# A fused linear-attention and windowed-attention stack on one core: the next rows turned inside an iteration's last products, the order of VectorE's and GpSimd's work rearranged, and a third pair of heads weighed by ScalarE in odd iterations

## What is computed

```python
xn = _layernorm(x)
# linear path, 16 heads of 32
q = softmax(_ln(xn) @ Wq + bq); k = softmax(_ln(xn) @ Wk + bk); v, p = split(_ln(xn) @ W_in)
k = (1 - smear) * k + smear * k_shifted_by_one_row
attn = tril(einsum(q, k) * decay);  o = (attn / (attn.sum(-1) + eps)) @ v
s = _ln(silu(p) * o @ W_out)
# window path, two layers, 8 heads of 64, windows of 128 rows
for l in range(2):
    h = shift_token(x); q, k, v = split(h @ wqkv[l]); q, k = rotary(l2norm(q), l2norm(k))
    x = x + softmax(q @ [k_before, k_own] + mask) @ [v_before, v_own] @ wo[l]
    h = _ln(shift_token(x)); a, g = split(h @ w1[l] + b1[l]); x = x + (a * gelu(g)) @ w2[l] + b2[l]
out = x0 + s * silu(x)
```

## Time and profile before

| | us |
|---|---|
| median of 3 runs | 2095.14 (2093.2 to 2096.72) |
| the profiled execution, device time | 2084.63 |
| its span, first to last instruction | 2082.8 |
| TensorE busy | 1938.6 (93%) |
| VectorE busy | 1791.2 (86%) |
| ScalarE busy | 1153.7 (55%) |
| GpSimd busy | 973.5 (47%) |

### The profile page before, as it was taken

How to read it: one execution, slowest core, us unless ns; L and a number is a source line. 1 busy time by engine, 2 the same in 40 slices (tenths; PEclk the granted TensorE clock), 3 DMA queues, 4 the chain that set the end, 5 groups by cost and what they waited for, 6 DMA issues and landing times.

```text
span 2082.8 us, 49017 instructions
## 1 busy us (share of the span) xinstructions
PE 1938.6 (93%) x15282; PEld 1668.4 (80%) x15282; DVE 1791.2 (86%) x5354; ACT 1153.7 (55%) x2734; POOL 973.5 (47%) x941
## 2 busy tenths in 40 slices
PE   5899999999999999999999999999999999999997
PEld 3788888888888888888787888877888778888786
DVE  6898898899898899889878888888988988888885
ACT  4465565566555556556545555555555655555553
POOL 3454544555554555554344434444444545344440
PEclk9999999999999999999999999999999999999998
DMA  5011000000000000100221011110111111111100
GB/s 191 18 31 31 19 29 25 28 20 30 28 19 25 30 19 29 30 19 30 69 64 37 28 36 33 30 40 27 36 35 29 34 33 30 35 31 32 38 22 24
DMA packets 81153, 72.78 MB, mean 35 GB/s; under 512 B 13484, under 2 KB 74344, under 8 KB 81096
## 3 DMA queue, kind: packets, MB, share of 16 engines
q1 hardware_dynamic: 81096, 72.05, 11.4%
HBM read 42.64 MB, written 16.78 MB: 29 GB/s over the span
## 4 chain that ended last, share of the span: by engine, by line
PE 47%; DVE 27%; issue 14%; POOL 8%; ACT 2%; DVEq 1%; SPq 0%; POOLq 0%; DMA 0%; ACTq 0%
PE bank L1403 31%; PE bank L1408 9%; PE bank L1415 6%; POOL inv_norm L648 6%; DVE prob L1002 4%; DVE prob L988 4%; ACT xT L767 2%; DVE sq_sum L1284 2%; DVE qk_sum L1296 2%; POOL k_carry L707 2%; DVE mix_work L1248 1%; DVE mix_work L1269 1%; DVE row_inv L997 1%; DVE row_min L988 1%; DVE h_n L1241 1%
## 5 line engine op out<-in xcount | busy, mean ns | idle before, releaser
L1403 PE MATMUL bank<-hT_n,w_s 128*128 128x128 f32 x3072 | 417.8, 288 | 17.5 <-ACT gel L888 16.8
L1403 PEld LDWEIGHTS bank<-hT_n,w_s 128*128 128x128 f32 x3072 | 379.2, 198 | 49.7 <-ACT gel L888 24.2
L798 ACT ACTIVATE prob<-prob,row_min 128x256 f32<-128x256 f32 x512 | 256.6, 503 | 160.9 <-DVE row_min L988 160.6
L1408 PE MATMUL bank<-wqkv_s,xT 128*128 128x512 f32 x1152 | 314.7, 408 | 15.7 <-DVE xT L1179 12.8
L691 POOL TENSOR_TENSOR rot_other<-raw,rot_t 128x256 f32<-128x256 f32 x256 | 187.7, 765 | 235.8 <-ACT raw L767 235.8
L648 POOL TENSOR_TENSOR inv_norm<-sq_clip,half_neg 128x16 f32<-128x16 f32 x64 | 218.4, 3412 | 91.4 <-DVE sq_clip L1287 91.3
L1408 PEld LDWEIGHTS bank<-wqkv_s,xT 128*128 128x128 f32 x1152 | 205.7, 190 | 67.3 <-DVE xT L1179 24.5
L988 DVE CUSTOM_DVE_ANT_0 prob<-bank,table,inv_norm 128x256 f32<-128x256 f32 x512 | 226.0, 478 | 2.3 <-issue 2.3
L1002 DVE TENSOR_SCALAR prob<-prob,row_inv 128x256 f32<-128x256 f32 x512 | 207.5, 447 | 9.1
L1403 PE MATMUL bank<-w_s,hid 128*128 128x256 f32 x768 | 195.2, 384 | 0.5 <-DVE hid L1332 0.5
L767 ACT ACTIVATE pT<-bank 128x512 f32<-128x512 f32 x256 | 145.0, 606 | 72.1 <-PE bank L1415 71.9
(11 more groups left out here) (182 smaller groups left out, 4261.5 us busy)
## 6 DMA issues: line engine op xcount, KB each, us to landing
k_prev<-k_carry SPq DMA_DIRECT2D x32, 224.0 KB, 2.5
x_s<-in_L_attn_x SPq DMA_DIRECT2D x32, 128.0 KB, 2.1
rot_s<-in_rotary SPq DMA_DIRECT2D x64, 64.0 KB, 2.0
rows_normalised<-xh SPq DMA_DIRECT2D x32, 128.0 KB, 1.7
y_n<-rows_normalised SPq DMA_DIRECT2D x32, 128.0 KB, 2.1
x_between_layers<-x SPq DMA_DIRECT2D x32, 128.0 KB, 1.7
s_between_passes<-s_out SPq DMA_DIRECT2D x32, 128.0 KB, 1.7
x_s<-x_between_layers SPq DMA_DIRECT2D x32, 128.0 KB, 2.1
```

The costliest lines, as they stand in the source:

```text
L798: ins = act.activation(prob[:, h, :], prob[:, h, :], ACT.Exp, bias=row_min[:, c:c + 1], scale=-1.0, accum_out=row_sum[:, c:c + 1])
L1403: return pe.matmul(out, lhsT, rhs, start=first, stop=last)
L1408: ins = pe.matmul(out, halved(left[:, a]), halved(right[:, b]), start=first and n == 0, stop=last and n == 2)
```

## The change

Seven edits, each in the order of one or more engines.

1. **Turned rows.** The transposes of the next unit's rows (`turn_x`), ScalarE's copies (`turned_x`, `turned_rows`) and VectorE's low halves (`low_turned_x`) move from the head of an iteration to the tail of the one before. On TensorE they stand ahead of the last products: in an even iteration ahead of the product with `wout_s`, in an odd one ahead of the last two `w2_s` products.
2. **Third pair of heads.** In odd iterations VectorE keeps only the reciprocal for `b0`; ScalarE multiplies (`weigh_b0`), two activations of 128x256, after the copies of `pT`.
3. **Final product.** VectorE's three instructions for `f` move from ahead of `weigh("a1")` to behind `scores("b1")`; in odd iterations the last of them moves further down.
4. **p ahead of exp.** VectorE adds the bias to p right behind `scores("b1")`, ScalarE's tanh goes ahead of its exponential of q and k.
5. **Half sums.** The softmax sums of k and of q are separate: k's stays, q's (`qsum`, `qeps`) goes behind `ql`.
6. **Inverse norm in two halves.** GpSimd computes 8 columns for k at the old place and the 8 for q, in odd iterations, behind `qdec`.
7. **Tails.** In odd iterations VectorE adds the shifted keys and forms `lb` ahead of `gated`; TensorE's first two `w2_s` products go behind the transposes of q; in even iterations `state_add` goes ahead of `residual`. On SyncE the two `k_prev` transfers go ahead of the output's.

```diff
@@ VectorE
                 if a is not None:
                     weigh("a1", a)
+                    if one is not None:
+                        inverse("b0", a)
...
+                if a is not None and one is None:
+                    weigh("b0", a)
                 if a is not None:
                     scores("b1", a, att_bank[0])
+                if one is not None:
+                    dve.wait_ge(mix_pe.sem, mix_pe.at("p", one))
+                    dve.tensor_tensor(p_lin, mix_bank[1][:, :], bias_mix[:, 1, :], ALU.add)\
+                       .then_inc(mix_dve.done("p"), 1)
+                if f is not None:
+                    finish_u(f)
+                    if one is None:
+                        finish_out(f)
...
-                    dve.tensor_reduce(qk_sum[:, :], heads(qk), AX_X, ALU.add).then_inc(mix_dve.done("sum"), 1)
+                    dve.tensor_reduce(qk_sum[:, MH:2 * MH], heads(qk[:, ME:2 * ME]), AX_X, ALU.add)\
+                       .then_inc(mix_dve.done("sum"), 1)
...
+                if u_next is not None and one is None:
+                    low_turned_x(u_next)
+                if one_next is not None:
+                    dve.wait_ge(mix_act.sem, mix_act.at("xt", one_next))
+                    low_x(xhT, mix_bank[0]).then_inc(rows_dve.done("xl"), 1)
@@ GpSimd
-                    root(inv_norm[:, p, :], sq_clip[:, :], 2 * H).then_inc(proj_pool.done("inv"), 1)
+                    root(inv_norm[:, p, H:2 * H], sq_clip[:, H:2 * H], H).then_inc(proj_pool.done("invk"), 1)
+                    if one is None:
+                        root(inv_norm[:, p, 0:H], sq_clip[:, 0:H], H).then_inc(proj_pool.done("invq"), 1)
@@ ScalarE
+            def weigh_b0(a):
+
+                s = list(STEP_HEADS).index("b0")
+                act.wait_ge(att_dve.sem, att_dve.at("rb0", a))
+                for j, h in enumerate(STEP_HEADS["b0"]):
+                    ins = act.activation(prob[:, h, :], prob[:, h, :], ACT.Copy, scale=row_inv[:, 2 * s + j:2 * s + j + 1])
+                ins.then_inc(weighed.done("nb0"), 1)
@@ TensorE
+                if u_next is not None and one is not None:
+                    turn_x(u_next)
                 if m is not None:
-                    if two is None:
-                        mlp_out(m, 2, 4)
                     mlp_out(m, 4, HC)
+                if u_next is not None and one is None:
+                    turn_x(u_next)
+                if one_next is not None:
+                    turn_rows(one_next)
                 if two is not None:
                     pe.wait_ge(mix_act.sem, mix_act.at("gt", two))
                     pe.wait_ge(mix_dve.sem, mix_dve.at("st0", two))
```

222 lines of the change are left out of this document (133 added, 89 removed).

## The result

The changed kernel takes 2033.88 us (median of 4 runs, 2025.98 to 2034.64) against 2094.17 for the kernel before beside it (4 runs, 2092.79 to 2096.72): a ratio of 0.9702, 95% interval 0.9687 to 0.9718. The profiled executions go from 2084.63 (span 2082.8) to 2033.74 us (span 2031.7), 51.1 us of span. The mean granted clock of TensorE is 0.984 in both profiled executions.

A forecast was written before the change was run, and what follows sets the result against it. TensorE (93% busy) and VectorE (86%) may both bound it, TensorE late only where VectorE's queue is. Gains of 1.2 and 2.1 us per first- and second-layer pair, times 16, made 53: 2095 - 53 = 2042 us, range 2012 to 2084.

The forecast's parts named there:

- I count 0 there: First layer, ahead of `wout_s`: the 0.66 us wait for the state sums only becomes one for `kl`, no change.
- The seam's 0.1: First layer, even to odd: VectorE's first scores come about 0.2 us later, costing a pair 0.1 us.
- The tail: First-layer odd tail: the 0.92 us wait for `lb` goes, `turn_k` waits a new 0.5, net gain 0.4 a pair.
- The seam's 1.1: Second layer, even to odd: `wout_s` and the norm of `y` start later, costing a pair 1.1 us.
- the new waits of the odd tail: Second-layer odd tail: final-product instructions beside GpSimd's subtraction push `la` and `ql`, costing 0.8 us a pair.
- Here the trade is bad: Even-to-odd turning: `turn_x` needs `kl`, with `wout_s` queued behind; the seam costs 1.1 us second layer, 0.1 first.
- The wait of 0.37 at the even heads: TensorE's wait for the low half of `xT` goes, worth 0.4 us a pair in both layers.
- 2.6 us off VectorE's way: Second-layer odd iterations, ahead of the k add: final product and `b0`'s weighing leave, the 1.37 us wait goes, +1.37.
- Gelu's start moves up: With tanh ahead of exp on ScalarE, gelu starts roughly 0.5 us earlier and TensorE's 0.50 wait goes: +0.5 a pair.
- rival 2: Only covers move at the seam; a stop at p over 1.5 us decides it: 11 us slower, 2106 us; chance 0.10.
- The clock is not in play: Pairs in both layers run at a granted clock of 1.00, so only TensorE's idle time, 106 us, can be won.
- Rival 1: GpSimd's power holds the port, delaying the `k_prev` sum up to 1.6 us; 42 of 53 us lost, 2084; chance 0.18.

The follow-up runs named there:

- e10: e5 with VectorE's add of p ahead of the final product's instructions and ScalarE's tanh ahead of exp: 2071.93 us, 0.9874 of the kernel before.
- e3: The changed kernel with the turning at the end of even iterations put behind the product with `wout_s`: 1990.76 us, 0.9516 of the kernel before.
- e13: e9 with the state's two additions in even iterations back behind the residual and the row norm: 2005.58 us, 0.9573 of the kernel before.
- e2: The changed kernel with x and the rows turned at the iteration heads again, in both kinds of iteration: 2003.51 us, 0.9551 of the kernel before.
- e5: The kernel before with only the final product's three VectorE instructions moved as in the changed kernel: 2072.53 us, 0.9905 of the kernel before.
- e11: e9 with the third pair of heads (`b0`) weighed by VectorE again in odd iterations: 1989.23 us, 0.9503 of the kernel before.
- e9: The changed kernel with the changes of e1 and e3 together: 1989.91 us, 0.9487 of the kernel before.
- e6: The changed kernel with the add of p and its tanh back at their old, later places: 2037.94 us, 0.9722 of the kernel before.
- e14: e10 with the low half of `oT` for heads 4 to 7 right behind the keys' add in odd iterations: 2052.29 us, 0.9804 of the kernel before.
- e12: e9 with the sums of q and k in one again and the queries' small terms behind it: 1994.59 us, 0.9535 of the kernel before.
- e8: The changed kernel with both halves of GpSimd's power at the old place in odd iterations: 2045.28 us, 0.9759 of the kernel before.
- e1: The changed kernel with ScalarE cutting the q weights ahead of turning x in iteration 0: 2026.15 us, 0.9698 of the kernel before.

## Why the prediction was right, and where it was not

- **The sum.** Forecast 53 us of gain to 2032 in the profile, measured 51 (2033.7). The mechanism was right in the main: VectorE's lateness made TensorE's waits, the waits of the earlier trace rows went, and the seam took part of it back. That the sum is this near is partly luck. Single terms were off in both directions, as told below. The forecast counted 16 pairs a layer, where 14 won in the first and 15 in the second; the two pairs of the layer change won nothing once the clock is taken out. And the clock gave back 11 us in the second layer and took about as much at the start and at the layer change.
- **The median.** Forecast 2042, measured 2033.88, 8 us less. The step that failed is "the median of the runs is 10.5 above the profile's time": the changed kernel's profiled execution, 2033.74, lies at its median. The runs of the kernel before beside e10 had a mean clock of 0.978 or 0.979, its profiled execution 0.984, and 0.005 of 2090 us is 10. So the profile showed the kernel before in a faster execution than most.
- **First-layer pair**, forecast 1.2, measured 1.06. The waits of the earlier trace rows went as said, 2.45 us of them. "I count 0 there" for the state against the low half of `kT` was right by rows (0.66 went, 0.60 came). The seam's 0.1 was too little; it cost 0.33. By my own terms the two pairs of transposes, 0.53, stood ahead of `wout_s` in this layer too, and I had carried on only 0.3 of them without a reason. The tail gave more: 0.92 went and 0.46 came.
- **Second-layer pair**, forecast 2.1 from 63.34, measured 2.57. The seam's 1.1 was 1.17 (e3 took back 1.26), the new waits of the odd tail 0.57 (0.42 and 0.15) instead of 0.8.
- **"Here the trade is bad"** holds, and more than I drew from it: without the even tail's turning the change gives 0.9516. The step that was mis-sized is the first layer's: I set the loss against the state's wait and called it 0.1, but e13 shows that the earlier additions win 0.91 a pair on their own, which the seam then gave away. The wait of 0.37 at the even heads was priced at 0.4 in both layers; e2 against e3 shows 0.05 in the first and 0.66 in the second.
- **"That is 2.6 us off VectorE's way [...] so the wait of 1.37 goes."** It goes with the finish alone (e5); the part of it that ScalarE's weighing was to bring is nothing (e11, tried in e9).
- **"Gelu's start moves up [...] +0.5."** The wait went, the gain did not come with it: 0.1 to 0.3 a pair (e10, e6). I added up the waits as if each were worth its length; in the odd half they stand one behind another on the same VectorE queue, as rival 2 put it, without its sign.
- **The odd tail.** The early low half of `oT` gives 0.24 and 0.69 (e14), the parted sum -0.10 and 0.59 (e12), the parted power 0.90 and -0.12 (e8). I gave the power no gain of its own but a sooner gate; what it brings in the first layer is an earlier row norm of the next x, which I had not traced.
- **"The clock is not in play"** was wrong: I had read one pair of the second layer, and half of them were of the other form. The layer change and the start had stretches at the lower clock as well.
- **Start and layer change** were not costed. I had read iteration 0's order as unchanged, but ScalarE's q weights went behind x (e1: 3.4 us of the start). Most of the rest is the clock by the estimate above, 6.6 us of the start and 4.4 of the layer change. The two pairs of the layer change took 134 to 142 us in the kernels here. Why the clock was lower there in one execution than in another is open.
- **Rival 1** is out: the keys' add took 0.68 or 0.69 us in all 32 odd tails, in 30 of them wholly inside the power. The Trainium skill, "SBUF — State Buffer", section "SBUF: two separate sides", would have it wait for the whole instruction; the measurement decides against it for the power. **Rival 2**'s stop at p was 1.2 us, under the 1.5 from which it would have decided.
- **Not accounted for.** The single gains do not add up: in the second layer e14's 1.6, the odd turning's 0.66 and the parted sum's 0.59 make 2.8 of the 3.8 us between the kernel before and e3. The power (-0.12) and the state's additions (0.06) change nothing in that, and some 1.0 us stays open. It may lie with the parts that were not tried alone (SyncE's order, the gated products behind the keys' add) or with what the parts do together. In the first layer the same sum is 0.34, 0.05, -0.10, 0.90 and 0.91, 2.1 of 2.26 us.

## What to carry to other kernels

Before you move work ahead of an instruction, ask what chain that instruction starts: here the product with `wout_s` headed a chain of 4.95 us, and 1.25 us put ahead of it cost 1.2 us in every pair, though TensorE did the same work. Waits of one engine for the same other engine's queue are not a sum to be won: take the chain from the last of them, since those ahead mostly pass on (0.81 and 1.37 us of waits taken away gave 0.56). Count what new waits come in, and what the moved instruction then runs beside: one product went from 0.42 to 2.02 us. And compare several turns of a loop before calling one typical; two forms of the same pair, 1.6 us apart, made 11 us here. Read the granted clock of a stretch before you look for a cause in the order of work there.
